# Two transformer blocks on one core: queries, keys and row maxima copied inside SBUF, a split start and a new step order

## The reference

```python
def block0(x, c, context):                       # a block with c as condition; LN over 128, 16 heads of 8
    c_proj = silu(c) @ W_mod + b_mod             # shift_a, scale_a, gate_a, shift_m, scale_m, gate_m
    qkv = modulate(_ln(x), shift_a, scale_a) @ W_qkv + b_qkv
    attn_w = softmax(einsum('bhqd,bhkd->bhqk', q, k) * scale)
    x = x + gate_a * (attn_w @ v @ W_proj + b_proj)
    q_c, kv_c = _ln(x) @ W_qc + b_qc, _ln(context) @ W_kvc + b_kvc
    x = x + softmax(q_c k_c^T * scale) v_c @ W_cproj + b_cproj
    x = x + gate_m * (gelu(modulate(_ln(x), shift_m, scale_m) @ W_mlp1 + b_mlp1) @ W_mlp2 + b_mlp2)
    ...
# block 1: the same three steps with adaLN (ln1, ln2, ln3), queries and keys turned by a rotary
# embedding, no gates, context without a norm, and a GELU MLP of 512
```

## Time and profile before

| what | us |
|---|---|
| median of 3 runs | 487.15 |
| lowest, highest | 484.03, 489.1 |
| the profiled execution | 482.83 |
| its span (first to last instruction) | 481.0 |
| PE busy | 402.3 (84%) |
| DVE busy | 329.8 (69%) |
| ACT busy | 267.8 (56%) |
| POOL busy | 158.9 (33%) |

### The profile page before, as it was taken

The page is one execution under the profiler, slowest core; times in us unless marked ns, Lnnn a source line. Parts: engine busy times, 40 slices in busy tenths (PEclk is TensorE's granted clock), DMA queues, the critical chain, the costliest instruction groups (busy, mean ns, idle before and its releaser), DMA issues.

```text
span 481.0 us, 10127 instructions
## 1 busy us (share of the span) xinstructions
PE 402.3 (84%) x3840; PEld 247.6 (51%) x3840; DVE 329.8 (69%) x841; ACT 267.8 (56%) x503; POOL 158.9 (33%) x138
## 2 busy tenths in 40 slices
PE   1855778899889979879888978989899998989696
PEld 1522444565565544544544534555565664747464
DVE  2666567899898963982974946878898994731331
ACT  1111265657666656465476556556565667576552
POOL 5762351651735520250241321335160542020130
PEclk9965699999999999998999989989999998999899
DMA  8860728285845631611613522545557472330001
GB/s 255 287 197 0 216 59 244 51 248 144 239 136 139 198 69 68 128 71 67 133 69 100 104 94 79 131 136 142 155 135 175 150 182 94 86 70 23 3 0 46
DMA packets 31272, 59.22 MB, mean 123 GB/s; under 512 B 3455, under 2 KB 7807, under 8 KB 30975
## 3 DMA queue, kind: packets, MB, share of 16 engines
q1 hardware_dynamic: 30935, 58.35, 44.1%
q10 hardware_dynamic: 288, 0.21, 0.1%
HBM read 31.81 MB, written 26.74 MB: 122 GB/s over the span
## 4 chain that ended last, share of the span: by engine, by line
PE 53%; DVE 16%; ACT 12%; POOL 10%; issue 5%; DMA 2%; SPq 1%; ACTq 0%; DVEq 0%; POOLq 0%
PE ps_ao L973 9%; POOL Kd L764 8%; PE ps_misc L999 7%; PE ps_sc L956 7%; DVE maxima L684 6%; PE ps_misc L875 6%; ACT PT L844 6%; PE ps_misc L918 5%; PE ps_misc L1019 4%; PE ps_misc L936 4%; PE ps_misc L879 4%; ACT xnT L830 3%; DVE xn L589 3%; PE ps_misc L1005 3%; POOL rstd L748 2%
## 5 line engine op out<-in xcount | busy, mean ns | idle before, releaser
L844 ACT ACTIVATE PT<-ps_sc 128x512 f32<-128x512 f32 (+1 forms) x256 | 138.9, 596 | 78.2 <-PE ps_sc L956 77.4
L684 DVE TENSOR_REDUCE maxima<-ps_misc 128x4 f32<-128x512 f32 (+1 forms) x256 | 154.1, 665 | 38.1 <-PE ps_misc L936 37.9
L764 POOL TENSOR_SCALAR Kd<-Kh,head_rows 128x512 fp32r<-128x512 f32 (+1 forms) x64 | 98.5, 1556 | 111.9 <-ACT Kh L804 82.4
L956 PE MATMUL ps_sc<-Qd,Ks 57*128 57x256 f32 (+1 forms) x512 | 64.6, 330 | 17.2 <-ACT PT L844 14.2
L973 PE MATMUL ps_ao<-PT,V 120*18 120x128 f32 (+1 forms) x2048 | 70.6, 277 | 2.8 <-ACT PT L844 2.7
L745 POOL TENSOR_SCALAR vareps<-mv 128x4 f32<-128x4 f32 (+1 forms) x28 | 6.8, 242 | 189.1 <-DVE mv L582 188.6
L956 PEld LDWEIGHTS ps_sc<-Qd,Ks 57*128 57x128 f32 (+1 forms) x512 | 37.7, 183 | 52.7 <-ACT PT L844 27.8
L830 ACT ACTIVATE xnT<-ps_misc,vec 128x128 f32<-128x128 f32 x80 | 30.1, 456 | 56.3 <-PE ps_misc L879 44.6
L973 PEld LDWEIGHTS ps_ao<-PT,V 120*18 120x18 f32 (+1 forms) x2048 | 50.3, 98 | 19.5 <-issue 8.1
L936 PE MATMUL ps_misc<-Kd,Qh 32*128 32x512 f32 (+1 forms) x256 | 42.2, 512 | 10.6 <-POOL Kd L764 8.8
L589 DVE TENSOR_SCALAR xn<-x,mv,rstd 128x128 f32<-128x128 f32 x96 | 36.5, 522 | 11.6 <-POOL rstd L748 11.6
(11 more groups left out here) (77 smaller groups left out, 471.2 us busy)
## 6 DMA issues: line engine op xcount, KB each, us to landing
Qd<-q_mem SPq DMA_DIRECT2D x64, 192.0 KB
k_mem<-Kh SPq DMA_DIRECT2D x16, 512.0 KB, 3.4
q_mem<-Qh SPq DMA_DIRECT2D x16, 512.0 KB, 2.9
Ks<-k_mem SPq DMA_DIRECT2D x32, 192.0 KB
Ks<-k_mem SPq DMA_DIRECT2D x32, 180.0 KB
k_mem<-Kl SPq DMA_DIRECT2D x16, 256.0 KB, 4.0
q_mem<-Ql SPq DMA_DIRECT2D x16, 256.0 KB, 3.0
W<-weights SPq DMA_DIRECT2D x1, 1792.0 KB, 18.5
```

Of the source, the lines that this page charges most:

```text
L684: dve.tensor_reduce(maxima[:, HG * n:HG * n + HG, st.b], bank(st.use + n)[:, 0:HG * ns].rearrange("p (h k) -> p h k", h=HG), AX_X, ALU.max ...
L764: pool.tensor_scalar(Kd[:, st.f % 2, c, 0:n], f32(Kh[:, st.f % 2, 0:n]), head_rows[:, c:c + 1], None, ALU.mult).then_inc(S["kd_ready"], 1)
L844: act.activation(PT[0:ns, st.k % PSLOTS, g, :, :, :].rearrange("p i e t -> p (i e t)"), ps_sc[0:ns, g, :], ACT.Exp, scale=SCALE).then_inc( ...
L956: ins = pe.matmul(ps_sc[0:ns, side, i * E * P:(i + 1) * E * P], Ks[rows, st.f % 2, n, st.b * ns:(st.b + 1) * ns], Qd[rows, st.f % 2, n, :, ...
```

## The change

- **Moves inside SBUF.** The stores to memory and the loads from it are gone. `khmove` and `qhmove` (4 DMAs each), `klmove` and `qlmove` (2 each) and `mmove` (2) copy the parts straight from `Kh`, `Kl`, `Qh`, `Ql`, `maxT` to their rows in `Ks` and `Qd`. Queries and keys are made in another order of features for this: `to_rows` copies the weights into that order in `Wr` (two on ACT, ten on POOL), and their biases and the rotary tables are loaded in it. `Kl` and `Ql` have two slots. Each move of unit f waits for its source and for all scores of unit f - 2.
- **Masks in four steps**, each with its own time (`kstep`), so other POOL work can stand between them.
- **First loads split.** The condition comes alone and first, then x of stream 0, then the two modulation matrices that the first `xT` needs; the other ten follow, with their products in a step of their own (`mods`). DVE fills half 0 of `Qd`, POOL fills `Ks` first, and `V` after the first `xn`, and the other half of `Qd` after the masks of unit 0.
- **More products ahead of waits.** `warm` also stands once ahead of `o`, `h2` and `yT`: 4 + 4 + 8 = 16 more products of that kind.
- **New step order.** Most numbers of `T` differ; one line:

```
-    kmask=(-28.83, -31.02, -29.69, -32.36),
+    kstep=(0.26, 0.83, 1.34, 0.25),
+    kmask=(-28.97, -31.14, -30.04, -32.48),
...
+    klmove=(0.82, 5.2, 2, 2),
+    qlmove=(-8.28, 0.64, 0.64, 0.64),
```

The core of the diff:

```diff
-WARM = 2
+WARM = {"xT": 2, "o": 1, "h2": 1, "yT": 1}
...
+RW = ["k0", "q0", "k1", "q1", "k2", "k2s", "q2", "q2s", "k3", "k3s", "q3", "q3s"]
+MODS = 2
...
-            at(front + T[x][a] + T[x + "hi"][a], Step(x + "hi", **who))
-            at(front + T[x][a] + T[x + "lo"][a], Step(x + "lo", **who))
-            at(front + T[x][a] + T[x + "lo"][a] + T[x + "store"][a], Step(x + "store", **who))
+            for part in ("hi", "lo"):
+                made = front + T[x][a] + T[x + part][a]
+                at(made, Step(x + part, **who))
+                at(made + T[x + part[0] + "move"][a], Step(x + part[0] + "move", **who))
         at(front + T["v"][a], Step("v", **who))
-        at(t + T["kmask"][a], Step("kmask", **who))
+        for c in range(HG):
+            at(t + T["kmask"][a] + c * T["kstep"][a], Step("kmask", h=c, **who))
...
-        at(t + T["mT"][a] + T["mstore"][a], Step("mstore", **who))
-        at(t + T["kload"][a], Step("kload", **who))
-        at(t + T["qload"][a], Step("qload", **who))
-        at(t + T["mload"][a], Step("mload", **who))
+        at(t + T["mT"][a] + T["mmove"][a], Step("mmove", **who))
...
+    rest = Step("mods")
+    rest.late = [st for st in plan if st.kind == "q" and st.f == 0][0].late
+    plan.insert([st.kind for st in plan].index("q") + 1, rest)
...
+        def to_rows(engine_copy, names):
+
+            for name in names:
+                engine_copy(w_rows(name).rearrange("p (c r n) -> p c r n", c=HG, n=NG),
+                            w(name).rearrange("p (n c r) -> p c r n", n=NG, c=HG)).then_inc(S["rows_made"], 1)
...
+                at, width = WCOLS["condT"]
+                sp.dma_start(first[:, at:at + width], weights[:, at:at + width]).then_inc(S["small_in"], 16)
                 load_x(0)
-                sp.dma_start(first, weights[:, 0:W_FIRST]).then_inc(S["small_in"], 16)
+                sp.dma_start(first[:, 0:MODS * D], weights[:, 0:MODS * D]).then_inc(S["mod_in0"], 16)
                 sp.dma_start(W[:, 0:W_SECOND - W_FIRST], weights[:, W_FIRST:W_SECOND]).then_inc(S["weights_in"], 16)
-                for s in range(1, STREAMS):
+                load_x(1)
+                sp.dma_start(first[:, MODS * D:at], weights[:, MODS * D:at]).then_inc(S["mod_in1"], 16)
...
+                for c in range(HG):
+                    sp.dma_start(cst[TROWS * c:TROWS * c + TROWS, P:NCONST],
+                                 by_rows(consts[:, P:NCONST], c)).then_inc(S["rope_in"], 16)
...
-                    if st.kind == "kstore":
-                        sp.wait_ge(S["k_high"], st.f + 1)
-                        sp.dma_start(k_mem[st.f, :, 0:3:2, :], f32(Kh[:, st.f % 2, :])[:, None, :].to_broadcast(
-                            [P, 2, CT])).then_inc(S[f"k_stored{st.f % 2}"], 16)
-                        sp.wait_ge(S["k_low"], st.f + 1)
-                        sp.dma_start(k_mem[st.f, :, 1, :], f32(Kl[:, :])).then_inc(S[f"k_stored{st.f % 2}"], 16)
-                    elif st.kind == "qstore":
-                        sp.wait_ge(S["q_high"], st.f + 1)
-                        sp.dma_start(q_mem[st.f, :, 0:2, :], f32(Qh[:, st.f % 2, :])[:, None, :].to_broadcast(
-                            [P, 2, CT])).then_inc(S[f"q_stored{st.f % 2}"], 16)
-                        sp.wait_ge(S["q_low"], st.f + 1)
-                        sp.dma_start(q_mem[st.f, :, 2, :], f32(Ql[:, :])).then_inc(S[f"q_stored{st.f % 2}"], 16)
...
+                    if st.kind in ("khmove", "klmove"):
...
+                        high = st.kind == "khmove"
+                        sp.wait_ge(S["k_high" if high else "k_low"], st.f + 1)
                         if st.f >= 2:
                             scored(sp, PAIRS * (st.f - 1))
...
+                            sp.wait_ge(S["fixed_ready"], 2)
+                        src = Kh if high else Kl
+                        for part in (0, 1) if high else (2,):
+                            for e in range(E):
+                                sp.dma_start(f32(Ks[ROW * e + part:P:E * ROW, st.f % 2, :, 0:n]),
+                                             f32(src[HALF * e:HALF * (e + 1), st.f % 2, 0:n])
+                                             ).then_inc(S[f"keys_in{st.f % 2}"], 16)
+                    elif st.kind in ("qhmove", "qlmove"):
+                        high = st.kind == "qhmove"
+                        sp.wait_ge(S["q_high" if high else "q_low"], st.f + 1)
...
                             scored(sp, PAIRS * (st.f - 1))
                         else:
...
+                            sp.wait_ge(*((S["zeros_ready"], 1), (S["fixed_ready"], 5))[st.f])
+                        src = Qh if high else Ql
+                        for part in (0, 2) if high else (1,):
+                            for e in range(E):
+                                sp.dma_start(f32(Qd[ROW * e + part:P:E * ROW, st.f % 2, e, :, :]),
+                                             f32(src[HALF * e:HALF * (e + 1), st.f % 2, :])
+                                             ).then_inc(S[f"queries_in{st.f % 2}"], 16)
+                    elif st.kind == "mmove":
                         sp.wait_ge(S["maxT_ready"], st.f + 1)
-                        sp.dma_start(m_mem[st.f].rearrange("h (b t) -> (h b) t", b=CB), f32(maxT[:, :])).then_inc(S["max_stored"], 16)
-                    elif st.kind == "mload":
-                        sp.wait_ge(S["max_stored"], 16 * (st.f + 1))
...
+                            sp.wait_ge(*((S["zeros_ready"], 1), (S["fixed_ready"], 5))[st.f])
+                        for e in range(E):
+                            heads = Qd[ROW * e + SPLIT:P:HALF, st.f % 2, e, :, :].rearrange("s n (b t) -> s (n b) t", b=CB)
+                            sp.dma_start(f32(heads), f32(maxT[GH * CB * e:GH * CB * (e + 1), :])
+                                         ).then_inc(S[f"maxima_in{st.f % 2}"], 16)
...
                 dve.memset(ps_ao[:, :], 0.0).then_inc(S["sums_zeroed"], 1)
-                dve.wait_ge(S["small_in"], 48)
-                dve.tensor_reduce(head_rows[:, :], ident.rearrange("p (n c d) -> p c n d", n=NG, c=HG), AX_XY,
-                                  ALU.add).then_inc(S["rows_ready"], 1)
+                dve.memset(f32(Qd[:, 0, :, :, :]), 0.0).then_inc(S["zeros_ready"], 1)
...
-                            modulation()
+                            modulation(0)
+                            dve.tensor_reduce(head_rows[:, :], ident.rearrange("p (c r n) -> p n c r", n=NG, c=HG),
+                                              AX_XY, ALU.add).then_inc(S["rows_ready"], 1)
+                    elif st.kind == "mods":
+                        modulation(1)
...
-                fill(1, V[:, :, :, :, :], 0.0)
-                fill(2, V[:, :, :, :, HD:VW], 1.0)
+                fill(1, f32(Ks[:, :, :, :]), 1.0)
...
-                            fill(3, f32(Ks[:, :, :, :]), 1.0)
-                            for half in range(2):
-                                fill(4 + half, f32(Qd[:, half, :, :, :]), 0.0)
+                            pool.wait_ge(S["xn_ready"], CB)
+                            fill(2, V[:, :, :, :, :], 0.0)
+                            fill(3, V[:, :, :, :, HD:VW], 1.0)
...
-                        for c in range(HG):
-                            pool.tensor_scalar(Kd[:, st.f % 2, c, 0:n], f32(Kh[:, st.f % 2, 0:n]),
-                                               head_rows[:, c:c + 1], None, ALU.mult).then_inc(S["kd_ready"], 1)
+                        if st.h == 0:
+                            pool.wait_ge(S["k_high"], st.f + 1)
+                            if st.f == 0:
+                                pool.wait_ge(S["rows_ready"], 1)
+                            if st.f >= 2:
+                                pool.wait_ge(S["max_taken"], GROUPS * (st.f - 1))
+                        pool.tensor_scalar(Kd[:, st.f % 2, st.h, 0:n], f32(Kh[:, st.f % 2, 0:n]),
+                                           head_rows[:, st.h:st.h + 1], None, ALU.mult).then_inc(S["kd_ready"], 1)
+                        if st.f == 0 and st.h == HG - 1:
+                            fill(4, f32(Qd[:, 1, :, :, :]), 0.0)
+                        if st.h == HG - 1 and st.f < 2:
+                            pool.wait_ge(S["rows_made"], 2 + 2 * st.f)
+                            pool.wait_ge(S[("weights_in", "rest_in")[st.f]], 16)
+                            to_rows(pool.tensor_copy, (RW[2:4], RW[4:])[st.f])
...
-                act.dma_start(cst[:, :], consts).then_inc(S["small_in"], 16)
...
                 act.activation(silu[:, 0, :], condT, ACT.Exp, scale=-1.0).then_inc(S["exp_done"], 1)
+                act.wait_ge(S["weights_in"], 16)
+                to_rows(lambda dst, src: act.activation(dst, src, ACT.Copy), RW[0:2])
...
-
-                    for _ in range(WARM):
```

(18 more changed lines are left out.)

211 lines of the change are left out of this document (104 added, 107 removed).

## The result

The changed kernel took 485.37 us (median of 16 runs, 483.26 to 489.35). The kernel before, run beside it, took 483.42 us (16 runs), which is 3.7 us under the median of the three runs that I started from. The ratio is 1.0062, with a 95% interval of 1.0033 to 1.0091. So the changed kernel is slower by 0.3 to 0.9%, within 1% of no change, and I had forecast 470 us, in a range of 459 to 481 us. Executions of the kernel before scatter from 478 to 489 us, at a mean granted clock between 0.96 and 0.93, so this ratio leaves out those over 1.5% above the fastest of their kernel (the medians of all give 1.004), and a difference of 1 or 2 us against the one profile of it says little. The span of the profiled execution is 483.0 us where that of before was 481.0.

The account below looks back on a forecast made before the run. From 80 us PE's list was taken as the bound, with DVE beside it to 160 us, before 57 us the wait chain. Terms -11 + 6 - 9 - 2 - 1.5 = -17.5 us took 487.15 to 470 us, range 459 to 481.

Parts of the forecast that it names:

- Start, -11 us: Up to the first score step: shorter loads, `xn` and modulation; worked 9.3 us earlier, taken as -11, ends -7 and -13.
- The stalls, 6.7 us: At the starts of units 1, 2 and 3 PE waits for late `mmove`: 2.8, 2.4 and 1.5 us, between 5 and 11.
- The stage from 80 to 160 us, +6: Attention 0: stalls 6.7, less idle time won 6.5, plus added warm products 5.8, gives +6 us.
- The rival: Stalls bigger than the order wins: landing 3.8 us, clock falls 1.7 us per stall, +13 instead of +6; 480 us; chance 0.15.
- 160 to 320 us, -9: Units in this stretch: five gains from (a) to (e) less 5.8 us of added products, -9 us, between -4 and -12.
- (a): 160 to 320 us: MLP 1/sigma behind two masks instead of four, so PE's 3.2 us wait for `xn` goes.
- (d): 160 to 320 us: two MLPs' eight passes took 5.38 us instead of 3.69; without the wait the clock stays, 3.4 us.
- (b): 160 to 320 us: a score step and a `norm` between `xT` and first `h` take most of 3.4 us; 3.0 counted.
- (c): 160 to 320 us: waits for exponentials, 4.7 us, lose about 3.
- (e): 160 to 320 us: 2 us of smaller waits go.
- 320 us and later, -3.5: From 320 to 400 us the order takes 2 of 5.2 idle us; from 400 us value steps and clock give -1.5.
- The one named for the order: Sign of proof: waits of score steps for exponentials down from 14 us to under 6.

Follow-up runs that it names:

- old order: Changed kernel, maxima first, with all plan numbers that both kernels have taken from before; masks still in four steps, products on: 472.69 us, ratio 0.9799.
- maxima first: Changed kernel with three plan numbers changed so the low moves of the next unit stand behind `mmove` on SP: 470.69 us, ratio 0.9787.
- mixed order: Changed kernel with `mmove` ahead of the next unit's low moves, no added products, new step numbers for attention 0 only, old ones elsewhere: 460.97 us, ratio 0.9565.
- kernel before with its maxima late: Kernel before, with the load of the maxima of units 1, 2 and 3 put behind the next unit's key load: 509.74 us, ratio 1.0629.

## Why the prediction was wrong, step by step

**Start, -11 us: the number right, in part by luck.** It came to -11.0 us. By its own steps I had the masks at 17.6 us and they came at 15.70, the masks of unit 1 ended at 42.4 instead of 44.7 us, and the first scores at 45.97 instead of 47.7; so the steps themselves were 1.7 us better than worked. The -11 that I took over the worked -9.3 came out by luck: its 1.7 us were for the masks of unit 2, for which PE was to wait less after an earlier start, and with the early start and the old order that wait is 2.8 us as before. It was the new order of attention 0 that took it to 0.6. The fill on DVE ended at 5.70 us, beside a fill on POOL from 0.88 to 4.39, and was not held by it. The Trainium skill (SBUF — State Buffer, section "SBUF: two separate sides") has the lock between VectorE and GpSimd only for VectorE instructions in a two-port performance mode or, against a GpSimd instruction that reads SBUF, with two inputs there. `xn` beside a fill behaves as under such a lock (7.17 and 3.58 us instead of 1.1), and two fills at a time, 3.47 and 3.51 us side by side, do not; in the prediction I had put the rule on the fill without its condition.

**The stalls, 6.7 us: place right, size 8.2 us.** An issue took 0.55 to 0.60 us and not 0.44, since the six stood at 1.14 to 1.18 us for two; the landing was 2.0 us and not 2.5; the cover at the first boundary was 1.9 us and not 2.1. The Trainium skill (DMA: Bandwidth & Descriptors, "Anatomy of one DMA") gives a DMA about 2 us fixed, in a section on DMAs that GpSimd issues, while here SP issues them; the trace has 2.00 all the same. It was the issues that I had too cheap.

**The stage from 80 to 160 us, +6: wrong, +15.0 in units 0 to 4.** The 15.0 us are 8.2 of stalls, 4.5 of slower products behind them, 0.4 won in units 0 to 3 otherwise (85.3 us with the maxima first, 85.8 before) and 2.7 lost in unit 4. So the term that failed is the price of a stall: I counted it at its length. That the clock falls behind it stood among the rivals, at 1.7 us a stall, and was left out of the sum; it measured 4.5 us in all. The rival had the right mechanism and a chance of 0.15. Its own sum was wrong too: three landings of 1.3 us more and three times 1.7 us are 9.0 us, so it should have said +15 and 482 us, not +13 and 480. That it would then have hit the +15.0 is partly luck, since the landing was 2.0 us and not 3.8.

That idle time won and work added nearly cancel (-6.5 + 5.8) did hold in units 0 to 3, but by another way than I gave: the new order won 3.9 us there, all in unit 0 (24.6 to 20.8 us), and nothing in units 1 to 3, where waits for `cnT` and the maxima (4.4 us) stand in for those for the exponentials (4.9 us, now 0.6). In unit 4 it did not hold: of the 2.7 us the products are 1.2 (23.0 against 21.8 us) and the new order 1.4 (23.0 against 21.6).

**160 to 320 us, -9: wrong, +0.7 in units 5 to 8.** Of its five gains these came: (a) the wait for `xn`, 2.6 of 3.2 us; (d) the clock, 1.00 instead of 0.97, with the eight passes at 3.70 us in three MLPs and in two parts of 1.98 and 1.88 us in the fourth; (b) the first `h` no longer waits. But (b) came back as 2.2 us ahead of a max step, (c) the waits for exponentials rose by 0.9 us instead of falling by 3, and of (e) the waits for `AOs`, `hT` and masks fell by 3.3 us while that for `attT` rose by 2.6.

The columns of the table put sizes on this. The mixed order has the steps of before in these units, no added products, and the masks apart: 128.8 us, 6.3 less than before, where I had put 6.6 for (a) and (d). The new order then costs 5.1 us (133.9), where I had put a gain of 8 for (b), (c) and (e). The products add 5.8 us of work, and 1.9 us of time (135.8). So what failed is the gain from the order, by 13 us, and 3.9 us of that were hidden because the products cost less than I had charged. The error was to look only at the pairs that the new order parted, and not at those it pushed together: `cT` and `k`, `aT` and `out`. The order of the steps was there to be read for both.

**320 us and later, -3.5: the number about right, its cause not shown.** Units 9 to 14 gave 2.7 us, the last stretch nothing. 1.5 of the 2.7 us are PE's busy time (127.5 and 126.0 us), and here the clock tells: unit 9 stood at 0.93 before and 1.00 after, unit 13 at 0.94 and 1.00 (29.1 and 27.9 us); 1.1 us are idle time. The kernel before with its maxima late, with the same list there, took 27.3 us for unit 13 at 1.00, and 26.1 for unit 9 at 0.87. So about half of this gain may be scatter.

**The sum.** In spans the forecast was -17.5 and the result +2.0 us. The 19.5 us between them are 9.0 in units 0 to 4, 9.7 in units 5 to 8 and 0.8 behind. Of the signs that I had named as proof those for the start and the masks did show (first scores at 46.0 us, `xn` at 1.1 us, the wait for `xn` and the slow `h` gone), and so did the stalls at three boundaries and no other; PE was busier, 409.0 against 402.3 us, but in a longer span. The one named for the order did not: the waits for exponentials went from 14.2 to 12.2 us and not under 6.

What stays open: whether one stall alone, without its neighbours, would lower the clock as much, since the two kernels with stalls both have three; what the moves inside SBUF are worth by themselves; why PE's busy time in units 5 to 8 is longer with the new attention steps at the same clock; and why the clock in unit 9 differs between kernels whose waits there are nearly the same.

## What to carry to other kernels

When a transfer moves to another place in a queue, look at what stands between its own wait and its issue: the price is that of everything ahead of it, their waits too, and on top of the stall itself the slower products behind it, here 0.4 to 0.55 of the stall again. When an order is changed, list the neighbours that it makes as well as those it parts, since a producer right ahead of its reader is a new wait on every round. And products put in to keep an engine busy are to be measured against none: here they cost 0.7% to 2% by the ratios in each of four kernels, and in none did the clock give that back.

## What the chip showed that I had not expected

- A stall of 3.6, 3.2 and 1.5 us in an engine that was nearly full had the granted clock at 0.90, 0.90 and 0.93 over the whole unit that followed, though with the maxima first the same units stood at 1.00 with waits of up to 1.1 us in them. It was still 1.00 in the first stall and 0.50 right behind it, when PE was busy again. In the kernel before with its maxima late, stalls of 5.95, 7.70 and 5.50 us had it at 0.83, 0.87 and 0.82: no lower for the longer one.
- A copy of 128 KB within SBUF, to 16 partitions, took 0.53 to 0.60 us of SP's time to issue and landed 2.6 us after the issue began; one of 16 KB took 0.53 to 0.55 us to issue and landed after 2.0 us. DMA moved 33.5 MB instead of 59.2 in the whole kernel, and I found no wait of PE that changed by it.
- A store to memory of 256 KB landed 6.5 us after its issue while loads of queries were under way, in the kernel before with its maxima late. That wait was hidden in the old order and came to light only when something needed stood behind it.
